# Triangle multiplication, four layers: the output gate evicted ahead of the roots, the low part on GpSimd, a shared scaling and a shorter lead

## The reference

```python
x = x + _L0_conv_ref(_gn(x), ...)
x = x + _L1_conv_ref(_gn(x), ...)
x = x + _L2_conv_ref(_gn(x), ...)
x = x + _L3_conv_ref(_gn(x), ...)
```

```python
xn = layernorm(x, norm_g, norm_b)
left = xn @ Wl.T * m * sigmoid(xn @ Wlg.T)
right = xn @ Wr.T * m * sigmoid(xn @ Wrg.T)
out_gate = sigmoid(xn @ Wog.T)
out = jnp.einsum('bikd,bjkd->bijd', left, right)
out = layernorm(out, out_norm_g, out_norm_b) * out_gate
return out @ Wout.T
```

## Time and profile before

| | |
|---|---|
| median of 3 runs | 2122.47 us (2121.59 to 2125.39) |
| the profiled execution | 2120.04 us, span 2118.1 us |
| TensorE matmul | 1768.2 us busy, 83% |
| VectorE | 1489.3 us, 70% |
| ScalarE | 1344.1 us, 63% |
| GpSimd | 805.5 us, 38% |
| DMA | 496.13 MB, mean 234 GB/s |
| mean granted TensorE clock | 0.959 |

### The profile page before, as it was taken

The page is one execution under the profiler, slowest core; times in us unless marked ns, Lnnn a source line. Parts: engine busy times, 40 slices in busy tenths (PEclk is TensorE's granted clock), DMA queues, the critical chain, the costliest instruction groups (busy, mean ns, idle before and its releaser), DMA issues. The chain is left out here.

```text
span 2118.1 us, 40561 instructions
## 1 busy us (share of the span) xinstructions
PE 1768.2 (83%) x10305; PEld 1040.4 (49%) x10389; DVE 1489.3 (70%) x3176; ACT 1344.1 (63%) x2413; POOL 805.5 (38%) x740
## 2 busy tenths in 40 slices
PE   0899996797998999965599799799799997799665
PEld 0445444685553444443255477644345444688332
DVE  7688886125753999995977388466489899344775
ACT  0587884455995787854599566478487876244322
POOL 0045445005990344445699300089000000000799
PEclk9999998998998999998899899999899999899999
DMA  7367776774995355546399666199456867653799
GB/s 322 132 199 231 246 237 208 284 313 155 365 366 179 121 173 181 175 138 236 132 347 367 234 221 206 43 327 393 150 181 213 263 214 222 248 238 158 258 358 336
DMA packets 326944, 496.13 MB, mean 234 GB/s; under 512 B 22827, under 2 KB 188462, under 8 KB 320438
## 3 DMA queue, kind: packets, MB, share of 16 engines
q1 hardware_dynamic: 326838, 494.93, 68.0%
HBM read 285.12 MB, written 197.13 MB: 228 GB/s over the span
## 5 line engine op out<-in xcount | busy, mean ns | idle before, releaser
L1327 POOL TENSOR_TENSOR shared<-O,out_rs 128x128 f32<-128x128 f32 (+1 forms) x128 | 92.1, 722 | 676.5 <-DVE out_rs L1227 675.5
L601 PE MATMUL ps<-w_heads,hi 64*128 64x256 f16 x3072 | 291.2, 272 | 39.5 <-DVE sig L752 27.2
L664 ACT ACTIVATE sig<-ps,largest 128x512 f32<-128x512 f32 x384 | 247.3, 692 | 51.5 <-PE ps L601 49.6
L1104 ACT ACTIVATE O<-ps 128x512 f32 (+1 forms) x144 | 151.7, 1053 | 189.2 <-PE ps L1025 189.2
L645 ACT ACTIVATE zs<-ps,shift 128x512 f32<-128x512 f32 x192 | 131.8, 686 | 183.3 <-PE ps L569 183.2
L601 PEld LDWEIGHTS ps<-w_heads,hi 64*128 64x128 f16 x3072 | 154.4, 94 | 187.5 <-DVE sig L752 71.5
L1371 PEld LDWEIGHTS ps<-ident,shared 128*128 128x128 f32 (+1 forms) x1024 | 118.8, 134 | 235.9 <-POOL shared L1327 141.5
L1371 PE MATMUL ps<-ident,shared 128*128 128x128 f32 (+1 forms) x1024 | 162.7, 284 | 79.3 <-POOL shared L1327 79.2
L601 PE MATMUL ps<-w_heads,lo 64*128 64x256 f16 x1536 | 212.7, 271 | 0.0
L569 PE MATMUL ps<-xs,center 128*128 128x512 f32 x384 | 202.3, 609 | 11.7 <-DVE r_terms L716 5.4
L752 DVE SCALAR_TENSOR_TENSOR sig<-ps,largest,sig 128x512 f32<-128x512 f32 x256 | 179.6, 742 | 38.0 <-ACT sig L664 36.5
(11 more groups left out here) (163 smaller groups left out, 3642.1 us busy)
## 6 DMA issues: line engine op xcount, KB each, us to landing
shared<-left_right SPq DMA_DIRECT2D x34, 2048.0 KB, 12.1
shared<-gate SPq DMA_DIRECT2D x224, 256.0 KB, 4.5
gate<-gates SPq DMA_DIRECT2D x96, 512.0 KB, 2.9
x_dram<-shared SPq DMA_DIRECT2D x192, 256.0 KB, 4.3
shared<-x_dram SPq DMA_DIRECT2D x192, 256.0 KB, 4.4
xs<-x_dram SPq DMA_DIRECT2D x64, 512.0 KB, 4.2
left_right<-stage SPq DMA_DIRECT2D x64, 448.0 KB, 5.7
left_right<-shared SPq DMA_DIRECT2D x64, 448.0 KB, 5.8
```

Source lines behind the costliest of these rows:

```text
L601: last = pe.matmul(PAIR[row][:, g, kb * S:kb * S + S], tokens[half, q % 8, at:at + P], k["w_heads"][half, part, :], start=(step == 0), sto ...
L664: act.activation(sig[:, slot, :].rearrange("p (c e) -> p c e", c=4), pair(row, 0), ACT.Sigmoid, scale=k["largest"][:, 0:1]).then_inc(c["si ...
L1104: act.activation(o_of(ch), ps[h % 4 // 2][:, h % 2, :].rearrange("p (b g i) -> p b g i", b=2, g=2), ACT.Copy).then_inc(c["o_copied"].sem, 1)
```

## The change

On ScalarE the gate's eviction moves ahead of `root_step`. In all three projections the subtraction that makes `lo` moves from VectorE's `norm` to a new `low_part` on GpSimd, two chunks ahead and in front of the chunk's masks; layer 3 gets a GpSimd program for it. Leads go from 16, 14, 13, 5, 4 to 14, 12, 11, 3, 2. In the output stage of layer 3 alone (`shares_scale`), the last chunk of each batch of 4 is scaled on ScalarE, in eight activations of 64 columns with a scale per partition, counted by a new counter `act_scaled`; `scaled` counts only GpSimd's. The mask functions are only indented anew.

```diff
@@ -450,7 +450,7 @@
 
 
 
-    LOAD, CENTER, VARIANCE, SPLIT, NORM = 16, 14, 13, 5, 4
+    LOAD, CENTER, VARIANCE, SPLIT, NORM = 14, 12, 11, 3, 2
     masked, gate = kind != "normed", a["gate"]
     with ExitStack() as ctx:
         def sb(name, shape, dt=F32):
@@ -674,11 +674,11 @@
                     square(i, q + CENTER, Z)
                 gate_pair(i, q, 0)
                 gate_pair(i, q, 1)
-                root_step(i, q, more)
                 act.wait_ge(c["gate_mm_done"].sem, c["gate_mm_done"](m + 1))
                 stored = c[f"gate_out{q % 4 // 2}"]
                 act.wait_ge(stored.sem, stored(i * 64 + q // 4 * 16))
                 act.activation(gates[:, q % 4, :], GATE, ACT.Sigmoid, scale=k["largest"][:, 2:3]).then_inc(c["gate_done"].sem, 1)
+                root_step(i, q, more)
 
             fold.root(act)
             act.wait_ge(fold.done.sem, fold.done(8))
@@ -730,12 +730,10 @@
                     dve.wait_ge(c["gate_mm_done"].sem, c["gate_mm_done"](m - 7))
                     dve.tensor_tensor(hi[:, q % 8, :], zs[:, q % 16, :], R, ALU.mult).then_inc(c["hi_done"].sem, 1)
                 dve.tensor_tensor(xn[:, q % 2, :], zs[:, q % 16, :], R, ALU.mult).then_inc(c["xn_done"].sem, 1)
-                dve.wait_ge(c["xn_done"].sem, c["xn_done"](m + 1))
                 if not masked:
+                    dve.wait_ge(c["xn_done"].sem, c["xn_done"](m + 1))
                     dve.wait_ge(c["gate_mm_done"].sem, c["gate_mm_done"](m - 7))
                     dve.tensor_copy(hi[:, q % 8, :], xn[:, q % 2, :]).then_inc(c["hi_done"].sem, 1)
-                dve.wait_ge(c["hi_done"].sem, c["hi_done"](m + 1))
-                dve.tensor_tensor(lo[:, q % 8, :], xn[:, q % 2, :], hi[:, q % 8, :], ALU.subtract).then_inc(c["lo_done"].sem, 1)
 
             def left_and_right(i, q):
 
@@ -768,45 +766,55 @@
...
+            def low_part(i, q):
+                m = i * BODY + q
+                pool.wait_ge(c["xn_done"].sem, c["xn_done"](m + 1))
+                pool.wait_ge(c["hi_done"].sem, c["hi_done"](m + 1))
+                pool.tensor_tensor(lo[:, q % 8, :], xn[:, q % 2, :], hi[:, q % 8, :], ALU.subtract).then_inc(c["lo_done"].sem, 1)
+
+            def step(i, q, more):
+                if more(NORM):
+                    low_part(i, q + NORM)
+                if paired:
+                    mask_rows(i, q)
+                elif masked:
+                    for row in range(ROWS):
+                        mask_pair(i, q, row)
+
+            for q in range(NORM):
+                low_part(0, q)
+            bodies_of(pool, step)
 
     fold.finish()
     for s in range(4):
@@ -1130,6 +1138,7 @@
     LOAD_X, LOAD_G = 4, 6 if gate_first else 5
     EVERY = 2 if kept is not None else 1
     RING = 4
+    shares_scale = n == 3
     with ExitStack() as ctx:
         def sb(name, shape, dt=F32):
             return ctx.enter_context(nc.sbuf_tensor(f"out_{name}_{n}", shape, dt))
@@ -1159,6 +1168,16 @@
             at = q % BATCH * 2 * ROWS
             return values[:, q // BATCH % BATCHES, :, at:at + 2 * ROWS, :].to_broadcast([P, 2, 2 * ROWS, H])
 
+        def scaled_by_act(q):
+
+            return shares_scale and q % BATCH == BATCH - 1
+
+        def scaled_by_pool(i, q):
+
+            if shares_scale:
+                return c["scaled"]((i * BATCHES + q // BATCH) * (BATCH - 1) + q % BATCH + 1)
+            return c["scaled"](i * BODY + q + 1)
+
         def bodies_of(eng, step):
 
             with eng.Fori(0, bodies - 1) as i:
@@ -1223,7 +1242,10 @@
                 batch = i * BATCHES + b
                 dve.wait_ge(c["ln_root"].sem, c["ln_root"](batch + 1))
 
-                dve.wait_ge(c["scaled"].sem, c["scaled"](batch * BATCH - (BATCHES - 1) * BATCH))
+                freed = batch - (BATCHES - 1)
+                dve.wait_ge(c["scaled"].sem, c["scaled"](freed * (BATCH - 1 if shares_scale else BATCH)))
+                if shares_scale:
+                    dve.wait_ge(c["act_scaled"].sem, c["act_scaled"](freed))
                 dve.reciprocal(rs[:, b % BATCHES].rearrange("p b t -> p (b t)"), std[:, b % BATCHES]).then_inc(c["ln_scale"].sem, 1)
                 dve.wait_ge(c["ln_scale"].sem, c["ln_scale"](batch + 1))
 
@@ -1340,7 +1362,7 @@
             def step(i, q, more):
                 if gate_first and more(CENTER):
                     center(i, q + CENTER)
-                if not gate_first and more(SCALE):
+                if not gate_first and more(SCALE) and not scaled_by_act(q + SCALE):
                     scale(i, q + SCALE)
                 if gate_first:
                     if more(SCALE):
@@ -1355,14 +1377,18 @@
                         scale(0, q - (CENTER - SCALE))
             else:
                 for q in range(SCALE):
-                    scale(0, q)
+                    if not scaled_by_act(q):
+                        scale(0, q)
             bodies_of(pool, step)
 
         @block.tensor
         def _(pe):
             def turn(i, q):
                 m = i * BODY + q
-                pe.wait_ge(c["scaled"].sem, c["scaled"](m + 1))
+                if scaled_by_act(q):
+                    pe.wait_ge(c["act_scaled"].sem, c["act_scaled"](i * BATCHES + q // BATCH + 1))
+                else:
+                    pe.wait_ge(c["scaled"].sem, scaled_by_pool(i, q))
                 free = c["gated"] if gate_first else c["wt_copied"]
                 pe.wait_ge(free.sem, free(m - 3))
                 for row in range(ROWS):
@@ -1413,6 +1439,18 @@
                     ins = act.activation(u[0:HH, q % RING], TURNED[q % 4], ACT.Copy)
                 ins.then_inc(c["wt_copied"].sem, 1)
 
+            def scale(i, q):
+                m = i * BODY + q
+                act.wait_ge(c["ln_scale"].sem, c["ln_scale"](i * BATCHES + q // BATCH + 1))
+                act.wait_ge(c["wt_done"].sem, c["wt_done"](m - 3))
+                for jb in range(2):
+                    for token in range(2 * ROWS):
+                        tokens = rows[:, jb, bass.ds(m * 2 * ROWS + token, 1), :].rearrange("p t h -> p (t h)")
+                        at = q % BATCH * 2 * ROWS + token
+                        last = act.activation(scaled[:, q % RING, jb, token, :], tokens, ACT.Copy,
+                                              scale=rs[:, q // BATCH % BATCHES, jb, at:at + 1])
+                last.then_inc(c["act_scaled"].sem, 1)
+
             def root(i, b):
                 batch = i * BATCHES + b
                 act.wait_ge(c["ln_stat"].sem, c["ln_stat"](batch * BATCH + BATCH))
@@ -1424,6 +1462,8 @@
             def step(i, q, more):
                 if more(TURN):
                     copy(i, q + TURN)
+                if more(SCALE) and scaled_by_act(q + SCALE):
+                    scale(i, q + SCALE)
                 if gate_first:
                     m = i * BODY + q
                     act.wait_ge(c["out_mm_done"].sem, c["out_mm_done"](m + 1))
@@ -1447,6 +1487,8 @@
                 act.wait_ge(c["u_cleared"].sem, c["u_cleared"](1))
             for q in range(TURN):
                 copy(0, q)
+            if shares_scale:
+                scale(0, SCALE - 1)
             bodies_of(act, step)
 
     for s in range(RING):
@@ -1460,7 +1502,10 @@
         c[name].advance(batches)
     if counted:
         c["aggregated"].advance(5)
-    for name in ("ln_stat", "scaled", "wt_done", "wt_copied", "out_mm_done", "x_new",
+    c["scaled"].advance(NCH - batches if shares_scale else NCH)
+    if shares_scale:
+        c["act_scaled"].advance(batches)
+    for name in ("ln_stat", "wt_done", "wt_copied", "out_mm_done", "x_new",
                  *(("centered", "gated") if gate_first else ("out_gated",))) + (("counted",) if counted else ()):
         c[name].advance(NCH)
```

More of the change, by code:

```diff
@@ L93, in build @@
             "tr_done", "tr_copied", "tri_done", "packed", "o_copied", "o_stored", "o_moved",
-            "ln_stat", "ln_root", "ln_scale", "centered", "scaled", "wt_done", "wt_copied", "gated",
+            "ln_stat", "ln_root", "ln_scale", "centered", "scaled", "act_scaled", "wt_done", "wt_copied", "gated",
             "out_mm_done", "u_cleared", "out_gated", "x_new", "counted", "aggregated")}
@@ new lines, in _, with mask_pair, mask_rows @@
+        @block.gpsimd
+        def _(pool):
+            def mask_pair(i, q, row):
+                m = i * BODY + q
+                b = q // SCH
+                if q % SCH == 0 and row == 0:
+                    pool.wait_ge(c[f"lr_out{b}"].sem, c[f"lr_out{b}"](i * 16 * SEG_PARTS))
+                    pool.wait_ge(c[f"first_out{b}"].sem, c[f"first_out{b}"](i * 64))
+                pool.wait_ge(c["pair_read"].sem, c["pair_read"](m * 2 + row + 1))
+                product = sig[:, (2 * q + row) % 4, :].rearrange("p (a e) -> p a e", a=4)
+                by_g = k["mask"][:].rearrange("p g b i -> p (g b) i")
+                mk = by_g[:, :, bass.ds(m * ROWS + row, 1)].to_broadcast([P, 4, P])
+                pool.tensor_tensor(staged(b, q, row), product, mk,
```

(18 more changed lines are left out.)

35 lines of the change are left out of this document (removed).

## The result

| | before | after |
|---|---|---|
| median | 2122.03 us (2120.24 to 2125.39, 4 runs) | 2097.19 us (2095.99 to 2099.36, 4 runs) |
| profiled execution, span | 2120.0, 2118.1 us | 2097.3, 2095.5 us |

What follows compares the result with a forecast made beforehand. TensorE's own work was taken to bound ordinary projection chunks, VectorE the tails, GpSimd the last output stage. 2120.0 us less 28.3 in the projections and 13 in the last stage gave 2079 us, range 2064 to 2103.

Steps and rivals of the forecast that it cites:

- likeliest case: Whole kernel: all parts work as forecast, 2079 us, reaching from 2071 to 2089 us; chance 0.55.
- rival (c): Relief smaller: subtraction near 1.8 us stretches GpSimd's tail, or an extra ScalarE table reload; 2095 to 2105 us, chance 0.12.
- (b): Last output stage: DMA bounds it at about 365 to 375 GB/s, only 5 us gained there, 2087 us; chance 0.20.
- 1.6 us of stall stays per root: Projections: with the gate first, TensorE's wait at each root moves elsewhere, and 1.6 us of it remains.
- rival (a): Roots: the reordering removes the stall, 21 roots give another 1.63 us each, 34 us, 2045 us; chance 0.07.
- 7 x (2.59 - 1.63) = 6.7: Second projection: seven roots fall from 2.59 to 1.63 us, as the low part no longer holds VectorE; 6.7 us gained.
- in the body GpSimd hides it and VectorE's relief earns nothing: Projection bodies: GpSimd's 3.3 us of masks and subtraction fit a 4.11 us chunk that TensorE bounds.
- The gain of the tails: Projection tails: without the low part VectorE's pitch falls over some seven chunks, gaining 1.2, 5.7 and 4.8 us.
- the first two go to GpSimd's 3.27 us: First and second projection tails: pitch per chunk falls from 3.44 and 4.07 us to GpSimd's 3.27 us.
- Rival (d): First two projections: GpSimd's queue sets the pitch once the subtraction passes 2.06 us; 2161 us at 2.7 us; chance 0.04.
- Loads keep their distance of two chunks from the centering, so no transfer comes later relative to its reader: Shorter lead: loads and centering both move by two chunks, so no input was expected late and no loss counted.
- two chunks move from the tail's pitch to the full one: Shorter lead: two chunks per projection go at 4.105 us instead of the tail's pitch, losing 1.3, 0.1 and 1.0 us.

Runs made afterwards that it cites:

- e8: The kernel after, with GpSimd's low part held until VectorE's split is done in the one step of eight that has a split: 2084.1 us, ratio 0.9838.
- e10: The kernel after with its low part held behind the split and all the old leads (16, 14, 13, 5, 4): 2083.7 us, ratio 0.9835.
- e1: The kernel before with nothing but the gate evicted ahead of the root step: 2123.8 us, ratio 1.0015.
- e11: The kernel before plus low part on GpSimd, held behind the split, and shared scaling; old order and old leads: 2082.5 us, ratio 0.9828.
- e2: The kernel before with only the low part moved to GpSimd: 2103.2 us, ratio 0.9919.
- e4: The kernel before with only the shorter leads: 2124.0 us, ratio 1.0010.
- e7: The kernel after with only the old leads (16, 14, 13, 5, 4) put back: 2096.2 us, ratio 0.9882.
- e9: The kernel after with its low part held behind the split and loads 16 chunks ahead, other leads short: 2081.4 us, ratio 0.9821.
- e3: The kernel before with only the last output stage's scaling shared with ScalarE: 2108.4 us, ratio 0.9944.

## Why the prediction was right, and where its steps were wrong

The time fell inside the range, and the sign was right. The likeliest case gave 41 us, and 24.8 came: 2097 us lies outside that case's own 2071 to 2089. The outcome is the total of rival (c), 2095 to 2105, but by other causes: its subtraction near 1.8 us was not there. Its aside, "VectorE and GpSimd slow one another", was. So the sign rests on terms that were there, the tails and the shared scaling, but that the range held the time is partly luck: the room had been left for (b) and (c), and the miss of the shorter lead was in neither. Of the 16 us missing, 9.5 lie at the split (e8) and about 9 in the lead; the tails gave about 2 us more than forecast.

**Gate ahead of the roots.** Right in its mechanism. "1.6 us of stall stays per root" is what e10 shows, 1.60, and rival (a) with its 34 us fell (e1). Wrong in the second projection: "7 x (2.59 - 1.63) = 6.7" assumed that nothing but the low part could hold the split. The roots there cost 3.0 us each in after, and the body grew by 2.6 us. The step that failed is "in the body GpSimd hides it and VectorE's relief earns nothing": GpSimd's time is hidden, but what it does to VectorE is not. The cast went from 0.41 to 1.09 us, which lengthens TensorE's pause from 1.64 to 2.09 us; with the clock of 0.54 behind it the gap is 7.63 and not 6.29 us, at every second root. e8 takes out the cause, and 9.5 us go with it. Over two chunks the gaps at a root are 9.8 us in the first projection and 10.3 to 10.4 in the fourth, as forecast, but 10.4 and 12.0 in the second.

The Trainium skill has the rule (SBUF — State Buffer, SBUF: two separate sides): VectorE in a two-port mode, or with two inputs in SBUF against a GpSimd operation that reads SBUF, and GpSimd share one pair of ports, whoever starts first keeps it for the whole instruction, and the other waits. By that rule the trace agrees: the cast ended 0.28 us after GpSimd's instruction, once the low part (after) and once a mask (e11). That the cast, with its one input, runs in a two-port mode is taken from the page; the trace does not show it. VectorE's products, 0.68 and 0.74 us with one input in PSUM, are not lengthened. The same rule would read the 1.528 and 0.692 us of the earlier trace rows, the low part with and without a mask on GpSimd. No run isolated that, but the timeline of before has the same sign, here in its second projection:

```profile
717.49 2.04 POOL L801 TENSOR_TENSOR stage<-sig,mask 128x1024 bf16<-128x1024 f32 x1 [2.03 <-DVE sig L752]
718.55 1.53 DVE L738 TENSOR_TENSOR lo<-xn,hi 128x512 f16<-128x512 f32 x1
```

The low part ends 0.55 us behind the mask, and 0.51 to 0.55 us behind it in every one of the 118 places of the first two projections where it starts beside one.

**The low part.** Taken as 1.27 us with a range of 1.0 to 1.6; it is 1.157. The gain of the tails was undersized: 11.7 us forecast, 13.5 in e2. The second tail gave 9.3 and not 5.7, because "the first two go to GpSimd's 3.27 us" was wrong: while the rings last TensorE runs at 2.5 us a chunk and GpSimd falls behind. Rival (d), with 2.06 us as its threshold, stayed far away.

The Trainium skill's statement that GpSimd is about 2x slower (GPSIMD Engine Reference, Engine selection) gave 1.38 us; 1.157 / 0.692 is 1.7x, and against the 1.528 us that it replaced in the second projection GpSimd is the faster one.

**Shorter lead.** This term missed by about as much as the split cost: the forecast had 3 x -3.7 + 1.3 + 0.1 + 1.0 = -8.7 us, and alone it gave +2.1 (e4), in after about 0 to +1 (e7), beside the split's wait 0 (e8 against e10). The lead-in's 3.7 us are there in the first projection (96.02 to 92.25). Two steps failed. First, "Loads keep their distance of two chunks from the centering, so no transfer comes later relative to its reader": the distance in chunks stayed, but not the time. A load beside the stores takes 5 to 9 us, and its reader now comes 1.6 us sooner after the slowest one's issue (6.52 for 8.15 us). Giving back two chunks to the loads alone (e9) returned 6.8 us of bodies. Second, "two chunks move from the tail's pitch to the full one" used the tail of before; with the tail that the same change makes, 2 x (4.105 - 2.51) = 3.2 us in the first projection. The tails of e8 are longer than those of e10 by 2.5, 3.0 and 2.2 us, 7.7 in all. 6.8 + 7.7 = 14.5, which is what the lead-ins and the rest give back: the total differs by 0.6 us.

**Shared scaling.** Forecast -13 with bounds -15 and -5, pitch 2.0, copies 2.6 us, near 390 GB/s; measured -11.9 alone (e3) and -14.1 in the stretch of after, 2.0, 2.7 and 398. Rival (b) fell: DMA does not stop at 365 GB/s.

By stretch, with the term each was forecast at, lead-in included: first projection -4.8, measured -3.8 + 6.4 = +2.6; second -16.0, measured -5.5 - 3.5 = -9.0; fourth -7.5, measured -3.4 + 1.3 = -2.1; last stage -13, measured -14.1. The measured ones include whatever the other stages in between varied by.

## What to carry to other kernels

Work moved to an idle engine is free only if it leaves the engine beside it alone: look for what that engine does in the short step on which everyone waits, and order the moved work behind it. A shorter lead only moves chunks from the tail to the body: it is worth the lead-in saved, less what a body chunk costs above a tail chunk, and the tail's pace to reckon with is the one after the change. Check a load's distance in microseconds and not in chunks: how long its slowest transfer takes beside the stores, and how soon its reader comes when the pauses that lay between them move.

## What was not expected of the hardware

A cast of 16x512 from float32 to bfloat16 on VectorE takes 0.41 us alone and 1.01 to 1.18 us in all seven roots of one projection, where it starts 0.25 to 0.42 us behind GpSimd's subtraction; where it starts 0.93 to 1.06 us behind it, 0.42 to 0.50 us. Such a delay costs time only where TensorE waits for the split: in the second projection of e2, in the old order, the split's second step took 1.52 us (in after 0.68) and ended 0.54 us behind the low part, and the gaps at the roots stayed at 5.81 to 5.90 us. TensorE's granted clock was 0.54 in the chunk behind a pause of 2.09 us, and 0.64 behind one of 2.34, but 1.00 behind one of 1.64 and in the chunk behind one of 2.02 us. Its length alone does not decide: in the second projection of e1 the clock is 1.00 from 712 to 716 us, behind a pause of 3.07 us, while behind one of 2.51 us the pair of centering matmuls took 1.62 us and not 1.02. What else decides stays open. The window of e1:

```profile
712.00:716.00 4.00, 3.93 (x32) 2.09 (x33) 3.96 (x6) 2.79 (x5) 2.04 (x1) 1.00 0.77 264
```
